# Second mixture of experts: all expert weights through the sync queue, and 24 unread products on TensorE ahead of the first block

## The reference, cut to what matters

```python
def _moe_forward(x, centroid, Wg, bg, W1, b1, W2, b2):
    xs = x.reshape(T, D)
    d2 = |xs|^2 + |centroid|^2 - 2.0 * (xs @ centroid.T)
    dist = jnp.sqrt(jnp.maximum(d2, 1e-12))
    w, sel = jax.lax.top_k(dist, K)
    w = jax.nn.softmax(w, axis=1)
    we = zeros(T, E).at[arange(T)[:, None], sel].add(w)
    for e in range(E):
        h = silu(xs @ Wg[e] + bg[e]) * (xs @ W1[e] + b1[e])
        out = out + we[:, e:e + 1] * (h @ W2[e] + b2[e])
```

## Time and profile before

| | |
|---|---|
| median of 3 runs | 871.26 us (871.09 to 873.1) |
| profiled execution, its own time | 877.44 us |
| its span, first to last instruction | 875.6 us |
| PE busy | 760.1 us (87%) |
| mean granted TensorE clock | 0.933 of full |
| second mixture's blocks | from about 668 to 868 us of the span |
| POOL: gathers of W1, gathers of W2 | 17 and 19 |

### The profile page before, as it was taken

How to read it: one execution, slowest core, us unless ns; L and a number is a source line. 1 busy time by engine, 2 the same in 40 slices (tenths; PEclk the granted TensorE clock), 3 DMA queues, 4 the chain that set the end, 5 groups by cost and what they waited for, 6 DMA issues and landing times.

```text
span 875.6 us, 13584 instructions
## 1 busy us (share of the span) xinstructions
PE 760.1 (87%) x4761; PEld 629.0 (72%) x4761; DVE 563.3 (64%) x1031; ACT 415.0 (47%) x896; POOL 284.2 (32%) x231
## 2 busy tenths in 40 slices
PE   6999999998988399989988988888978988888894
PEld 3588888888944387479964766676558877778783
DVE  3369999998359799176665666765365644454540
ACT  4544444442342299254443565666472544453440
POOL 0074544440016234300033022240312454554632
PEclk9999999999999699879999999997876999998998
DMA  6400000000240000000007674350432689888862
GB/s 243 173 1 18 18 18 18 18 1 0 84 191 0 0 2 2 1 0 1 10 0 176 156 169 106 108 144 21 156 134 68 190 236 231 238 225 241 237 157 67
DMA packets 33610, 84.51 MB, mean 97 GB/s; under 512 B 8566, under 2 KB 24406, under 8 KB 30215
## 3 DMA queue, kind: packets, MB, share of 16 engines
q0 software_dynamic: 13584, 42.51, 17.8%
q1 hardware_dynamic: 19959, 41.13, 15.8%
HBM read 73.23 MB, written 10.38 MB: 95 GB/s over the span
## 4 chain that ended last, share of the span: by engine, by line
PE 56%; DVE 13%; issue 7%; ACT 4%; DMA 2%; POOL 1%; POOLq 0%; SPq 0%; DVEq 0%; ACTq 0%
PE PS L468 52%; DVE RW L1752 2%; PE PS L1011 1%; DVE SM L2050 1%; DVE WK L1812 1%; PE PS L640 1%; DVE WK L1809 1%; DVE RO L1755 1%; DMA KST<-mask_rows 1%; PE PS L857 1%; PE PS L981 1%; ACT SQ L1056 1%; ACT RO L1189 0%; POOL OT L1551 0%; DVE M L2059 0%
## 5 line engine op out<-in xcount | busy, mean ns | idle before, releaser
L1466 POOL TENSOR_TENSOR PRODL<-RW,PRODH 128x361 fp32r<-128x361 f32 x64 | 64.9, 1017 | 114.0 <-ACT PRODH L1123 110.4
L468 PE MATMUL PS<-CTXH,WKV0H 128*128 128x362 f32 x256 | 86.4, 338 | 9.6 <-DVE RW L1708 9.0
L2050 DVE TENSOR_REDUCE SM<-PS 100x1 f32<-100x362 f32 x128 | 64.8, 531 | 44.5 <-PE PS L468 43.8
L468 PE MATMUL PS<-RB,HTT 114*128 114x256 f32 (+1 forms) x240 | 65.4, 429 | 27.3 <-issue 24.8
L468 PE MATMUL PS<-CTXL,WKV0H 128*128 128x362 f32 x256 | 84.7, 331 | 0.0
L468 PE MATMUL PS<-CTXH,WKV0L 128*128 128x362 f32 x256 | 84.3, 329 | 0.0
L468 PEld LDWEIGHTS PS<-RB,HTT 114*128 114x128 f32 (+1 forms) x240 | 50.0, 214 | 38.7 <-issue 31.0
L1312 ACT ACTIVATE WK<-PS 120x400 f32<-120x400 f32 (+1 forms) x96 | 48.4, 507 | 40.9 <-PE PS L468 40.0
L468 PEld LDWEIGHTS PS<-CTXH,WKV0H 128*128 128x128 f32 x256 | 48.7, 190 | 15.9 <-DVE RW L1708 11.1
L468 PE MATMUL PS<-KST,QST 97*100 97x362 f32 x128 | 53.2, 428 | 6.3 <-DMA KST<-mask_rows 3.4
L1755 DVE TENSOR_REDUCE RO<-RW 128x100 f32<-128x400 f32 x64 | 56.2, 878 | 2.2
(11 more groups left out here) (314 smaller groups left out, 2041.1 us busy)
## 6 DMA issues: line engine op xcount, KB each, us to landing
KST<-keys_by_head SPq DMA_DIRECT2D x24, 362.0 KB
keys_by_head<-KTHL SPq DMA_DIRECT2D x8, 724.0 KB, 3.4
CTX<-ctxT SPq DMA_DIRECT2D x16, 361.0 KB, 6.7
RB<-W SPq DMA_DIRECT2D x2, 1368.0 KB
RW<-WGU SPq DMA_DIRECT2D x1, 2304.0 KB, 8.6
RW<-WKV SPq DMA_DIRECT2D x1, 2048.0 KB, 9.8
RQ<-W SPq DMA_DIRECT2D x1, 1368.0 KB
RW<-WD SPq DMA_DIRECT2D x1, 1152.0 KB, 10.2
```

The costliest lines, as they stand in the source:

```text
L468: return pe.matmul(out, lhsT, rhs, start=start, stop=stop)
L1466: pool.tensor_tensor(low, raw, high, ALU.subtract).then_inc(sem["a_products_low_ready"], 1)
L2050: dve.tensor_reduce(SM1[:, q % 2, j:j + 1], PS[0:S, i % 2, 0:KVE], AX_X, ALU.max, negate=True).then_inc(sem["c_maximum_found"], 1)
```

## The change

SP loads all weights. A new `load_weights(k)` and `load_down(k)` issue plain transfers of 128 rows; for blocks 8 to 19 the expert's number is read from SBUF (OWNED) into a register (`value_load`), once for each transfer. SP issues W1 of blocks 1 and 2 without waiting for the mixed heads and for its own earlier loads, W2 of blocks 0 and 1 ahead of the mixture, W1 of block 3 after `gu_low` of block 0, and then, in step k, W1 of block k + 4 after `gu_low(k + 1, 1)` and W2 of block k + 1 after `down1(k - 1)`. POOL keeps the row gathers and the scatters. `down1` reads 115 of the 128 rows as before. DVE writes OWNED in place of WROW.

PE gets 24 products of 342 columns, into PSUM bank 4, whose results are not read: 14 in front of the wait for `router_result_ready` 4, 2 between the wait for the WEIGHED products' operands and those products, 8 behind them and in front of `turn_tokens(0)`.

```diff
-            load(RAW[0], t["W1"][0:P], "moe1_small_loaded")
+            load_weights(0)
             sp.wait_ge(sem["c_turned_scores_summed"], 12 * (B - 1))
-            sp.wait_ge(sem["moe1_small_loaded"], 48)
-            sp.wait_ge(sem["c_heads_mixed"], 4 * (B - 1))
-            for k in (1, 2):
-                load(RAW[k], t["W1"][k * P:(k + 1) * P], "moe1_small_loaded")
+            load_weights(1)
+            load_weights(2)
...
+            def expert_rows(table, k):
+                if k < E1:
+                    return table[k * P:(k + 1) * P]
+                e = sp.value_load(OWNED[0:1, k - E1:k - E1 + 1], min_val=0, max_val=E1 - 1)
+                return table[bass.ts(e, P)]
...
+            load_down(0)
+            load_down(1)
+            sp.wait_ge(sem["expert_weights_low_ready"], N0 + 2)
+            load_weights(3)
...
+            for k in range(NBLK - 1):
+                if k + 4 == E1:
+                    sp.wait_ge(sem["router_result_ready"], 9)
+                if k + 4 < NBLK:
+                    sp.wait_ge(sem["expert_weights_low_ready"], N0 + 2 * (k + 1) + 2)
+                    load_weights(k + 4)
+                if k:
+                    sp.wait_ge(sem["down_summed"], N0 + k)
+                    load_down(k + 1)
...
+            def idle_products(n):
+                pe.wait_ge(sem["expert_weights_low_ready"], N0 + 2)
+                for _ in range(n):
+                    mm(PS[:, 4, 0:HH], GUH[0][:, 0, 0, 0:P], GUH[0][:, 1, 0, :], True, True)
+
+            idle_products(14)
             pe.wait_ge(sem["router_result_ready"], 4)
...
             pe.wait_ge(sem["router_result_ready"], 7)
+            idle_products(2)
             for i in range(2 * B):
                 m = mm(PS[:, 7, 96:96 + 2 * NBLK], POSITION[:, i, :], WEIGHED[:, i, :, :], i == 0, i == 2 * B - 1)
             m.then_inc(sem["router_scores_summed"], 1)
+            idle_products(8)
...
                 if k + 3 < NBLK:
                     gather_rows(k + 3)
-                if k and k + 3 < NBLK:
-                    pool.wait_ge(sem["expert_weights_low_ready"], N0 + 2 * k + 2)
-                    gather_weights(k + 3)
                 if k:
                     add_rows(k - 1)
-                    if k + 1 < NBLK:
-                        gather_down(k + 1)
```

More of the change, by code:

```diff
@@ L219, in program @@
         SHIFT, BLOCK, TOKEN = ROUTE[:, 112:120], ROUTE[:, 120:120 + NOV], ROUTE[0:S, 132:140]
-        LANE, UNITROW, FIRST = ROUTE[:, 140:141], ROUTE[:, 141:142], ROUTE[:, 142:150]
-        STATIC, PICKED = ROUTE[:, 150:158], ROUTE[:, 158:166]
+        UNITROW, FIRST = ROUTE[:, 141:142], ROUTE[:, 142:150]
+        PICKED = ROUTE[:, 158:166]
         STARTS, EMPTY = ROUTE[:, 166:166 + NBLK], ROUTE[:, 186:186 + NBLK]
@@ L228, in program @@
         VACANT, OFFSET = TMP[:, 244:244 + NBLK], TMP[:, 264:272]
-        WROW = part("WROW", [P, NBLK], "RB", at_ + 856, U32)
+        OWNED = part("OWNED", [P, NOV], "RB", at_ + 856, U32)
         TROW = part("TROW", [P, NBLK], "RB", at_ + 880, U32)
@@ L444, in _, with load_weights, load_down @@
                 load_keys(b + 3)
+            def expert_rows(table, k):
[3 more added lines that the diff above has]
+                return table[bass.ts(e, P)]
+            def load_weights(k):
+                load(RAW[k % 3], expert_rows(t["W1"], k), f"weights_loaded{k % 3}")
+            def load_down(k):
+                load(DOWN[k % 2].rearrange("p t c -> p (t c)"), expert_rows(t["W2"], k), f"down_loaded{k % 2}")
             load(ROUTE, t["route"], "moe1_small_loaded")
-            load(RAW[0], t["W1"][0:P], "moe1_small_loaded")
+            load_weights(0)
             sp.wait_ge(sem["c_turned_scores_summed"], 12 * (B - 1))
-            sp.wait_ge(sem["moe1_small_loaded"], 48)
-            sp.wait_ge(sem["c_heads_mixed"], 4 * (B - 1))
-            for k in (1, 2):
-                load(RAW[k], t["W1"][k * P:(k + 1) * P], "moe1_small_loaded")
+            load_weights(1)
+            load_weights(2)
             sp.wait_ge(sem["c_turned_scores_summed"], 12 * B)
-            sp.wait_ge(sem["moe1_small_loaded"], 80)
+            sp.wait_ge(sem["moe1_small_loaded"], 32)
             load(BRAW, t["b1g"], "moe1_small_loaded")
-            load(DOWN[0], t["W2"][0:P].rearrange("p (t c) -> p t c", t=6), "moe1_small_loaded")
+            load_down(0)
+            load_down(1)
+            sp.wait_ge(sem["expert_weights_low_ready"], N0 + 2)
+            load_weights(3)
             sp.wait_ge(sem["rows_copied"], 4)
@@ L1015, in down1 @@
                 pe.wait_ge(sem["hidden_high_ready"], N0 + 2 * k + 2)
+                pe.wait_ge(sem[f"down_loaded{k % 2}"], 16 * (k // 2 + 1))
                 if k:
-                    pe.wait_ge(sem[f"down_loaded{k % 2}"], 16 * ((k + 1) // 2))
                     pe.wait_ge(sem["rows_out_ready"], k)
@@ L1343, in weights_there @@
             def weights_there(k):
[L1344 to L1347, removed]
+                act.wait_ge(sem[f"weights_loaded{k % 3}"], 16 * (k // 3 + 1))
             def gu_high(k, j):
@@ L1416, in hidden_high @@
                                                              x=3)).then_inc(sem["hidden_high_ready"], 1)
-            act.wait_ge(sem["moe1_small_loaded"], 112)
+            act.wait_ge(sem["moe1_small_loaded"], 48)
             act.wait_ge(sem["zeros_set"], 7)
@@ L1536, in mask_queries @@
                                        ALU.mult).then_inc(sem["c_query_slots_ready"], 1)
[L1538 to L1541, removed]
             pool.wait_ge(sem["zeros_set"], 6)
@@ L1564, in _ @@
             pool.memset(HTT1[96:P, 0, :], 1.0).then_inc(sem["zeros_set"], 1)
[L1565 to L1568, removed]
             def gather_rows(k):
@@ L1584, in add_rows @@
                                         YO[:, k % 2, :], None, compute_op=ALU.add).then_inc(sem["rows_added"], 16)
-            pool.wait_ge(sem["expert_weights_low_ready"], N0 + 2)
-            gather_weights(3)
-            gather_down(1)
             pool.wait_ge(sem["rows_stored"], 16)
@@ L1596, in _ @@
             for k in range(NBLK + 1):
-                if k + 3 == E1:
-                    pool.wait_ge(sem["router_result_ready"], 9)
                 if k + 3 < NBLK:
                     gather_rows(k + 3)
-                if k and k + 3 < NBLK:
-                    pool.wait_ge(sem["expert_weights_low_ready"], N0 + 2 * k + 2)
-                    gather_weights(k + 3)
                 if k:
                     add_rows(k - 1)
-                    if k + 1 < NBLK:
-                        gather_down(k + 1)
         @block.vector
@@ L2093, in _ @@
                 if q == 24:
-                    dve.wait_ge(sem["moe1_small_loaded"], 48)
-                    dve.tensor_copy(PICKB[:, 0:E1], PICKED)
-                    dve.tensor_copy(WROW[:, 0:E1], STATIC).then_inc(sem["router_result_ready"], 1)
+                    dve.wait_ge(sem["moe1_small_loaded"], 32)
+                    dve.tensor_copy(PICKB[:, 0:E1], PICKED).then_inc(sem["router_result_ready"], 1)
                 if q == -2:
@@ L2204, in owners @@
                 link(dve.tensor_scalar(OWNER, OWNER, E1 - 1.0, None, ALU.min))
-                dve.tensor_scalar(WROW[:, E1:NBLK], OWNER, float(P), LANE, ALU.mult,
-                                  ALU.add).then_inc(sem["router_result_ready"], 1)
+                dve.tensor_copy(OWNED[:, :], OWNER).then_inc(sem["router_result_ready"], 1)
                 dve.tensor_scalar(PICKB[:, E1:NBLK], OWNER, UNITROW, None,
@@ L2369 @@
     route[0:S, 132:140] = np.arange(B) * S + np.arange(S)[:, None] + 1
-    route[:, 140] = np.arange(P)
     route[:, 141] = -1.0
@@ L2373 @@
     route[:, 142:150] = P * np.arange(E1)
-    route[:, 150:158] = P * np.arange(E1) + np.arange(P)[:, None]
     route[0:E1, 158:166] = route[32:32 + E1, 158:166] = np.eye(E1)
```

## The result

The changed kernel takes 838.08 us (median of 4 runs, 837.28 to 839.77) against 872.18 us for the kernel before (871.09 to 873.42): ratio 0.9611, 95% interval 0.9589 to 0.9633, faster by 34 us. The forecast was 843, range 836 to 858. The profiled execution took 837.28 us, with a span of 835.0. Ratios and medians leave out executions in a slower state; one of 2402.16 us in `r_after` is such.

A forecast was written before the change was run, and what follows sets the result against it. PE, 87% busy, bounds the kernel, with gaps from late W2 gathers on five engines. 877.4 - 33 (loop) + 2 (products) = 846.4 for the profiled execution; between 846 and 840 for the median, 843 was taken, range 836 to 858.

The forecast's parts named there:

- W2's gather on five engines: Block loop: 115 rows lie on five engines, 23 on each, at 135 GB/s; 128 rows would use 16.
- SP issues W2 in time, value_load is free: Block loop: W2 lands in 9.5 us of 12.0 left, margin 2.5; value_load costs 0; 2 us of new waits allowed.
- The gain in the loop: Block loop and its end: waits, half-clock pieces and last down1 sum to 34.9 us, taken as 33.
- The terms of 23.8 and 7.5 us: Block loop: 23.8 us of PE waits before down1, and 7.5 us from TensorE's clock halving after long waits.
- The tail: Last down1: released late by its W2 and run slowly, 1.9 + 1.7 = 3.6 us to win.
- Profile and median: Median 6.2 us below profiled execution: 846 if these are loop waits, 840 if elsewhere; middle taken, 843.
- The products: Router to block 0: the 24 products lose 2 us net, bounds 4 lost and 4.5 won; the 8 return 1.2.
- The sign named for the front: Block 0's first product comes about 3 us later than 667.85, at a clock already rising.
- B: Block loop: transfers stay a partial bound at 290 GB/s, block 8.4 us, 853 us; needs share 0.85 or more; chance 0.17.
- D: Block loop: 236 GB/s is the engines' true mixed rate, blocks grow by 0.4 us, 879 us; chance 0.05.
- C: Block loop: the scatter becomes the bound, landing still 8.4 us, block 8.7 us, 858 us; chance 0.14.
- E: Router onward: the products work, clock full, 4.5 us won for 2 lost, 836.5 us; chance 0.07.

The follow-up runs named there:

- r_after: The changed kernel timed once more, on one chip with the same kernel without the 24 products: 838.87 us, ratio 0.9598 to the kernel before.
- e3_gather_128: Kernel before, weights still gathered by POOL in the old order, with the W2 gather over 128 rows instead of 115: 839.00 us, ratio 0.9604.
- e4_plain_115: Changed kernel with the plain loads of W2 taking 115 rows instead of 128: 902.10 us, ratio 1.0334 to the kernel before.
- the 120 and 125 rows: Kernel before with the gather of W2 over 120 or 125 rows instead of 115: 840.80 us (ratio 0.9603) and 884.33 us (1.0122).
- e7_scatter_wait: Changed kernel with rows_out(k) waiting for the scatter of block k - 1 instead of k - 2: 840.04 us, ratio 0.9589 to the kernel before.
- e1_loads_only: Changed kernel without the 24 unread products, all weights still loaded by the sync queue: 836.13 us, ratio 0.9583 to the kernel before.

## Why the prediction was right, and where its sizes were off

- **W2's gather on five engines.** Right, and the cause by itself: `e3_gather_128`, `e4_plain_115` and the 120 and 125 rows decide it. I had two causes in the argument, the lateness of the request on POOL and the uneven split. The first is real but has slack once the gather is fast: in `e3_gather_128`, asked for at the old place, the gathers land in 7.4 us.
- **SP issues W2 in time, value_load is free.** Right: landing after 7.5 us where I had estimated 9.5, and no wait for a load at all in blocks 8 to 19. The 2 us of new waits that I let stand did not come.
- **The gain in the loop.** Mis-sized. From block 0's first product to the end of the last `down1` it went from 867.75 - 667.85 = 199.9 us to 828.10 - 667.97 = 160.1, so 39.8 us, where the sum had 34.9. The terms of 23.8 and 7.5 us hold, but each interruption costs more than the wait before it: an unbroken piece of 14 + 12 products takes 4.79 us, the same pieces with a wait between 2.20 + 2.83 = 5.03. That is 0.24 us at each of 13 waits, 3.1 us. The tail gave 4.8 us instead of 3.6: from the start of its last 14 products to the end of the last `down1` it took 867.75 - 854.07 = 13.7 us before and 828.10 - 819.17 = 8.9 after. In it lies one more wait, behind the 150 us of the earlier trace rows and ahead of the last `down1`, which neither term had counted (chain of the kernel before):

```profile
854.07 2.21 PE PS L468 x14
856.28 1.02 issue
857.30 2.84 PE PS L468 x12
```

- **Profile and median.** Half of the 6.2 us by which the profiled execution lay above the median was put outside the loop. As far as two single executions tell, nearly all of it was in what the change removes: 877.44 became 837.28, 40.2 us less, while the medians went from 872.18 to 838.08, 34.1 less. By the prediction's own rule for that case the forecast was 846, 8 us above what came, since the loop's gain was put too low. The 3 us taken off for the median hid part of this: that the forecast of 843 is only 5 us off is luck to that extent.
- **The products.** The costs were right (2.3 for the 8, 0.7 for the 2, against 2.3 and 0.6). The 1.2 us that the 8 were to give back do not show: the products of block 0 are at full spacing 3.8 to 4.5 us after its start in the six traces with the 8, and 3.2 to 6.2 us in the eight without, in the mean 4.3 and 4.2. The 14 were hidden, and ran at full clock, which I had not expected: they started as soon as the scores ended, and the clock had not fallen by then (the last section). Net 2 us lost against the kernel without them: as forecast. The sign named for the front failed, though: block 0 began at half clock, not at a rising one, and 0.1 us later than in the kernel before, not 3. That trace had run its CENTS, RTH and NAMED products at half clock (3.99, 1.71 and 3.59 us; 2.91, 0.98 and 2.20 after), and the 2.8 us by which the operands of WEIGHED came earlier paid for the 2 and the 8.
- **The rivals.** B (a partial bound by the transfers) and D (slower, from 236 GB/s as the true rate) are out: 286 GB/s with no wait. B's own sign, a share of 0.85 or more, did come (0.86) without its effect. C (the scatter) is out with a landing of 7.0 us and the slack shown by `e7_scatter_wait`; POOL waited for `out` at 9 of 20 scatters, 43.6 us in all, and PE felt nothing of it. E, the clock full from the router on, did not come. The forecast sign that scatters land under 7.8 us held for the median, 7.0, not for the longest, 8.2.

## What to carry to other kernels

Look at a transfer while it is alone: here its DMA share of 0.32, beside a loop at 0.87, gave the uneven split away, and a row count with a large divisor up to 16 (13 rows that nobody reads were added) was worth 34 us, and moving all weights to another queue as well some 3 more, within the intervals. Products that only keep the clock up belong where PE waits anyway; put ahead of work whose operands are there, they cost their full length, and at half clock twice that. Before a long chain is called the next bound, count how late its result may come, not how long it takes.

## What was not expected of the hardware

- In kernels without any added product the clock often rises during the turning of the residual. In `e1_loads_only` PE, after 3.70 us of idling, did 9 RTH products and 16 turning ones, nothing else, and these stretches show it:

```profile
653.00:655.00 2.00, 2.00 (x11) 1.96 (x10) 1.79 (x8) 1.09 (x2) 0.00 (x0) 0.50 0.00 0
...
656.00:658.00 2.00, 1.15 (x9) 1.06 (x9) 1.97 (x4) 1.66 (x2) 0.00 (x0) 1.00 0.23 67
```

  In the kernel before and in `e3_gather_128` the same work left it at half; in the five other traces without the 14 the NAMED products behind it ran at full clock (2.2 to 2.4 us). With the 14 in front, the clock of the changed kernel was 1.00 up to the turning, 0.50 in it and 1.00 again before the NAMED products, so what the 14 win is lost during the turning, as the prediction had it, and comes back:

```profile
650.86:651.36 0.50, 0.50 (x9) 0.50 (x8) 0.43 (x3) 0.48 (x2) 0.00 (x0) 1.00 0.01 2
...
652.36:652.86 0.50, 0.50 (x5) 0.47 (x4) 0.43 (x3) 0.43 (x1) 0.00 (x0) 0.50 0.12 33
...
655.36:655.86 0.50, 0.00 (x0) 0.00 (x0) 0.50 (x1) 0.50 (x2) 0.00 (x0) 1.00 0.00 0
```

  The Trainium skill ("TensorE: Matmul & The Clock Gate", PE-mode transpose) has transposes not count as busy. The rises speak against that for these products of 128 x 100 float32, and the measurement decides; the fall inside the turning would fit it. What sets either off stays open.
- Whether the 14 products find the clock full is not theirs to say. In six traces with them they did (2.45 us, and 2.91 for the 32 CENTS products ahead); in `e4_plain_115`, with the same code up to there, the clock had fallen and they took 4.34 us, and CENTS 3.76. In the traces without them CENTS took 3.74 to 3.99 us. CENTS runs ahead of the 14, so they cannot be what keeps it fast. That they hold the clock is thus possible, and not shown.
- The gather of W2 over 120 rows, 15 engines by the rule of the divisor, ran at 243 GB/s with a share of 0.87, the one over 128 rows at 365 with 0.98: less per engine if the shares count busy engines (243 / 13.92 = 17.5 GB/s, 365 / 15.68 = 23.3), and still fast enough. No run tells why.
